# A selective scan's input products: the opening 128 tokens of a chunk by one full-array product

## The chip, the cores and the metric

The kernel runs on one core of one Trainium2 chip. The metric is the device time of one execution in microseconds (us), from three runs of the kernel before; the time of a changed kernel is compared with it. TensorE (PE) multiplies into PSUM, VectorE (DVE) runs the scans, ScalarE (ACT) the exponentials and copies, GpSimd (POOL) elementwise products and indirect transfers, SyncE (SP) issues the plain DMAs.

## What is computed

Input x is 2 x 2048 x 256, float32. Two layers, each with a layernorm ahead and a residual around it:

```
xn = layernorm(x)
B_t, C_t = xn W_B^T, xn W_C^T                 # 16 states n
dt  = softplus(xn W_dt1^T W_dt2^T + b)        # 256 channels d
A   = -exp(log_A);  A_bar = exp(dt * A)       # d x n
B_bar = (A_bar - 1) / (A + 1e-8) * xn * B_t
h_t = A_bar * h_(t-1) + B_bar                 # a scan over 2048 tokens for each d, n
y_t = sum_n h_t * C_t + D_skip * xn
x   = x + y
route = softmax(layernorm(x) Wr + br); e = argmax     # 8 experts
x   = x + gelu(layernorm(x) W1[e] + b1[e]) W2[e] + b2[e]
```

The kernel scans a shifted state, so that the input of its scan is w_t = u_t - u_(t+1), where u_t = xn_t * B_t[n]; a factor 1/(A + 1e-8) goes on C.

## The kernel before

The tokens are eight chunks (q = 0 to 7) of 512, four to a sequence; a chunk is four tiles (k = 0 to 3) of 128 tokens. Work in a chunk goes by sixteen units (n = 0 to 15); a unit m = 16q + n is two states of one half (128) of the channels, and thus two items g = 2m and 2m + 1, each 128 channels x 512 tokens. A unit passes these stages:

- `make_band` (POOL, L648): for each pair of units it multiplies a constant band (1 on the diagonal, -1 beside it, 65 wide, one for each 64 tokens) by the rows of B, for two states: 128 x 520, one operation. There are three such buffers.
- `make_w` (PE, L1055): w of the unit, 128 channels x (512 tokens x 2 states), in two PSUM banks. The stationary operand is xn of the tokens, the moving one the band. Each product covers 64 tokens, `product(r, k)`, where r is the upper or lower half of the array's rows, and writes 130 columns: two of them belong to the 64 tokens that follow, so they are added into PSUM on top of another product. Those with r = 0 use rows 0 to 63, those with r = 1 rows 64 to 127. `make_w(m, 0)` has five products (one of two columns alone), `make_w(m, 1)`, which waits for the end of the first part, has four: nine for a unit, each a float32 product of two instructions.
- `exp_a` (ACT, L835), A_bar of an item; `scan` (DVE, L1336), the recurrence, item by item, which reads w.
- multiplication with C (`make_hc`), on one of two engines: for a pooled item ACT copies C with its scale (`copy_C`, L825) and POOL multiplies (L667); for the others DVE does both in one operation from PSUM (L1355), a *VectorE pair*. `VECTOR_UNITS` lists which n of each chunk are VectorE pairs; sixteen of 128 units before.
- `add_y` (PE, L1093): four transposing products for each item, added up in PSUM (`YY`) over all items.

The four PSUM banks of `WW` hold two units, so PE's order in a chunk is, for each n: what `hops(q)` lists for n (small products for the next chunk, the router, or the skip term), then `make_w(m + 2)`, then `add_y` of the unit before the last. `make_w(m + 2)` waits until unit m's scans (or its VectorE pair) have freed the banks. All engines work through their queues in order.

`hops(q)` is a table: `xn0`, `xn1`, `bcd`, `brow`, `dt2_0`, `dt2_1` prepare chunk q + 1; `cbt`, `u_a`, `u01`, `u23` make the skip term; `xnr0`, `xnr1`, `routeT`, `route` the router of the chunk before; `early0`, `early1` (L1020) the token lists of the first four chunks, from which the first expert tiles are gathered while the last chunk still runs. `ODD`, `BANK` and `BEFORE` give each its shared PSUM bank and whose reader it has to wait for.

On SP, `chunk(q)` spreads a row of C over 128 partitions for every unit (`spread_C`, L497), six buffers ahead; in the last chunk at n = 9 it waits for `early1` and then issues three loads of W2 (L535), 512 KB each.

After the scan stage come 36 expert tiles (`hidden` L1172, `outputs` L1209), which are bound by PE alone.

Of the kernel before, what the change touches and what calls it, by code (L numbers as in the profile page):

```python
# [29 lines left out]
VECTOR_UNITS = [(4, 8, 12)] + [(5, 12)] * 4 + [(8,)] * 2 + [(4, 10, 15)]  # L30
# [9 lines left out]
BAND = 2 * (HALF + 1)  # L40
NR, NA, NH, NHC, NCS, NW, NB = 3, 4, 8, 8, 3, 4, 6
# [17 lines left out]
SMALL = dict(ident=P, logA=KD * N, wr=KD * CS, umask=1, wcd=KD * CBD, wdt2=D, skip=D, band=HALF + 1, last=1,  # L59
# [13 lines left out]
ODD = ("u01", "xn0", "bcd", "dt2_0", "dt2_1", "rank", "spread", "early0", "early1")  # L73
# [6 lines left out]
def hops(q):  # L80
# [121 lines left out]
def build(nc, x, small, w1, w2, b2, out):  # L202
    with ExitStack() as ctx:
# [38 lines left out]
        band_at = NR * TI * BAND  # L242
# [25 lines left out]
        bands = [b2_sb[:, i * TI * BAND:(i + 1) * TI * BAND].rearrange("p (i t) -> p i t", t=BAND) for i in range(NR)]  # L268
# [79 lines left out]
        most = max(b - a for a, b in BATCHES) * TI  # L348
# [3 lines left out]
        where = sb("where", [P, 3, most])  # L352
        lane = sb("lane", [P, 1])
# [117 lines left out]
        def _(eng):  # L471
# [28 lines left out]
            def chunk(q):  # L500
                for n in range(N):
# [75 lines left out]
        def _(eng):  # L577
# [184 lines left out]
        def _(eng):  # L762
# [75 lines left out]
            def emit(q):  # L838
                first, last, at = q == 0, q == NQ - 1, hops(q)
                for n in range(N):  # L840
# [23 lines left out]
                    if not first and n == (13 if last else 14):  # L864
                        softmax_exp(q - 1)
# [66 lines left out]
        def _(eng):  # L932
# [111 lines left out]
            def make_w(m, part):  # L1044
# [7 lines left out]
                def product(r, k, at=0, width=BAND, start=False):  # L1052
# [3 lines left out]
                                      band[rows, k, at:at + width], start=start, stop=not start, skip_group_check=True)  # L1056

                if part == 0:
# [7 lines left out]
                    product(0, 0, start=True)  # L1066
# [184 lines left out]
        def _(eng):  # L1251
# [178 lines left out]
            def place_tokens(batch, parts=(0, 1)):  # L1430
# [8 lines left out]
                if 0 in parts:  # L1439
# [418 lines left out]
```

## Time and profile before

| what | value |
|---|---|
| median of three runs | 726.18 us (724.6 to 726.65) |
| the profiled execution's own time | 726.01 us |
| its span, first to last instruction | 724.3 us |
| PE busy | 682.5 us, 94% |
| DVE, ACT, POOL busy | 538.0, 482.6, 485.6 us |
| mean granted clock of TensorE | 0.98 of full speed |

The span is one execution; busy time is what an engine's instructions took together, and a busy PE includes the latency of its pipeline. The scan stage takes the first 445 us or so, the experts the other 279 us. Granted clock 1.00 is TensorE at 2.4 GHz, 0.50 is 1.2 GHz. A view of the trace by windows has, in each row, the window (us from the span's start), its length, the busy us of the engines with the number of their instructions in brackets (in the order PE, PE's weight loads, DVE, ACT, POOL, or PE alone where a row is of one line's matmuls), the granted clock, the DMA engines' busy share and GB/s. The chunks are cut at the start of the w of a chunk's third unit, which is the first that PE makes within that chunk. In a group by line stand the busy us, the mean ns of one, and the idle time before them with what ended it.

### The profile page before, as it was taken

To read this page: it belongs to the slowest core of one execution; us is meant where nothing else is said; L and a number is where in the kernel's file an instruction comes from. 1 tells how busy PE (TensorE), PEld (TensorE's weight loads), DVE (VectorE), ACT (ScalarE), POOL (GpSimd) and SP (SyncE) were. 2 spreads that over 40 slices of the span, in tenths; PEclk is the share of its full clock that TensorE was granted. 3 is DMA by queue.
4 is the path that set the end of the run, shared out by engine and by line. 5 is a ranking of instruction groups with operands and counts; after the bars stand their busy time and mean duration, and the time that the engine had idled before them with its cause. 6 is when DMAs were issued, how large, how long until landed. Compare 5 with 4: busy or idle time off the path is not lost.

```text
span 724.3 us, 17510 instructions
## 1 busy us (share of the span) xinstructions
PE 682.5 (94%) x5826; PEld 574.6 (79%) x5827; DVE 538.0 (74%) x950; ACT 482.6 (67%) x1005; POOL 485.6 (67%) x616
## 2 busy tenths in 40 slices
PE   8899799999999998899998989999999999999997
PEld 7777677777787776678776778898999999977776
DVE  7799889989989989999999878887343333344441
ACT  3887999998998997899998586433232323233451
POOL 3889998998998987989989587233343434343331
PEclk9699999999999999999999799999999999999999
DMA  6787542342343243143242077711111111111010
GB/s 235 269 258 254 204 145 78 104 148 93 108 152 117 82 137 107 60 148 117 83 125 88 30 256 240 277 41 49 58 52 59 48 58 45 58 38 33 25 45 16
DMA packets 42290, 82.21 MB, mean 114 GB/s; under 512 B 4824, under 2 KB 12637, under 8 KB 42208
## 3 DMA queue, kind: packets, MB, share of 16 engines
q1 hardware_dynamic: 37600, 68.58, 28.7%
q0 software_dynamic: 4608, 12.59, 5.4%
q8 instruction: 45, 0.74, 0.4%
q14 instruction: 37, 0.30, 0.1%
HBM read 69.35 MB, written 13.37 MB: 114 GB/s over the span
## 4 chain that ended last, share of the span: by engine, by line
PE 58%; ACT 12%; POOL 9%; issue 7%; DVE 2%; DMA 1%; SPq 0%; POOLq 0%; ACTq 0%; DVEq 0%
PE WW L1172 16%; PE misc L1209 15%; PE WW L1055 10%; POOL w_sb L667 7%; PE YY L1093 7%; ACT w_sb L835 5%; ACT Csb L825 5%; PE misc L1204 2%; PE WW L1166 2%; DMA w_sb<-c_rows 1%; PE YY L1141 1%; PE misc L969 1%; ACT xin L805 1%; PE misc L981 1%; DVE w_sb L1336 1%
## 5 line engine op out<-in xcount | busy, mean ns | idle before, releaser
L667 POOL TENSOR_TENSOR w_sb<-w_sb,Csb 128x512 f32<-128x512 f32 x224 | 282.7, 1275 | 41.9 <-DVE w_sb L1336 37.7
L1055 PE MATMUL WW<-b_sb,xin 64*128 64x130 f32 (+2 forms) x2304 | 203.3, 293 | 23.4 <-DVE w_sb L1336 12.5
L1055 PEld LDWEIGHTS WW<-b_sb,xin 64*128 64x128 f32 x2304 | 168.4, 192 | 70.3 <-issue 30.6
L1336 DVE TENSOR_TENSOR_SCAN w_sb<-WW,hlast,w_sb 128x512 f32<-128x512 f32 x170 | 210.1, 1269 | 13.5 <-issue 6.5
L835 ACT ACTIVATE w_sb<-dt,negA 128x512 f32<-128x512 f32 x256 | 169.5, 709 | 4.0 <-DVE w_sb L1336 2.0
L916 ACT ACTIVATE dt<-WW,b1c 128x128 f32<-128x128 f32 x256 | 72.8, 387 | 129.2 <-PE WW L1172 129.0
L1093 PE MATMUL YY<-sm,w_sb 128*128 128x128 f32 x1024 | 142.4, 284 | 6.2 <-DVE row L1384 4.3
L729 POOL DMA_INDIRECT y_out<-CbX,ocol x36 | 42.6, 1184 | 142.0 <-DVE CbX L1758 137.3
L1093 PEld LDWEIGHTS YY<-sm,w_sb 128*128 128x128 f32 x1024 | 113.4, 143 | 21.2 <-issue 4.3
L825 ACT ACTIVATE Csb<-w_sb,invA 128x512 f32<-128x512 f32 x150 | 102.5, 713 | 23.2 <-POOL w_sb L667 21.5
L1209 PE MATMUL misc<-w_sb,dt 128*128 x512 | 115.7, 379 | 0.5 <-issue 0.5
L1209 PEld LDWEIGHTS misc<-w_sb,dt 128*128 128x128 f32 x512 | 94.9, 190 | 12.4 <-issue 0.7
L1172 PE MATMUL WW<-z,xin 128*128 128x128 f32 x512 | 99.2, 275 | 0.2
L1172 PEld LDWEIGHTS WW<-z,xin 128*128 128x128 f32 x512 | 78.4, 192 | 1.6 <-issue 0.7
L648 POOL TENSOR_TENSOR b_sb<-sm,brow 128x520 f32<-128x520 f32 x64 | 67.9, 1061 | 6.6 <-ACT brow L777 6.6
L1336 DVE TENSOR_TENSOR_SCAN w_sb<-WW,w_sb 128x512 f32<-128x512 f32 x54 | 63.8, 1208 | 7.2 <-ACT w_sb L835 3.5
L1758 DVE TENSOR_TENSOR CbX<-CbX,misc 128x256 f32<-128x256 f32 x36 | 15.1, 420 | 70.5 <-PE misc L1209 63.5
L825 ACT ACTIVATE Csb<-CbX,invA 128x512 f32<-128x512 f32 x74 | 50.8, 714 | 15.6 <-POOL w_sb L667 15.6
L1172 PE MATMUL WW<-z,xnT 128*128 128x128 f32 x288 | 55.9, 276 | 0.9 <-issue 0.9
L1172 PEld LDWEIGHTS WW<-z,xnT 128*128 128x128 f32 x288 | 44.5, 192 | 2.0 <-issue 1.5
L1172 PE MATMUL WW<-z,Csb 128*128 128x128 f32 x224 | 43.3, 275 | 0.0
L1638 DVE COPY z<-YY 128x256 f32<-128x256 f32 x34 | 14.3, 422 | 32.1 <-PE YY L1141 31.8
(304 smaller groups left out, 817.7 us busy)
## 6 DMA issues: line engine op xcount, KB each, us to landing
w_sb<-c_rows SPq DMA_DIRECT2D x86, 256.0 KB, 3.3
CbX<-c_rows SPq DMA_DIRECT2D x42, 256.0 KB, 3.3
w_sb<-w_in SPq DMA_DIRECT2D x20, 512.0 KB, 5.7
token_rows<-row SPq DMA_DIRECT2D x8, 1024.0 KB, 4.6
w_sb<-w_in SPq DMA_DIRECT2D x24, 256.0 KB
xin<-x_in SPq DMA_DIRECT2D x8, 512.0 KB, 3.8
w_sb<-x_in SPq DMA_DIRECT2D x7, 512.0 KB, 7.9
b_sb<-b_in SPq DMA_DIRECT2D x1, 780.0 KB, 8.3
```

What stands on the lines that cost most here:

```text
L648: eng.tensor_tensor(bands[pair % NR].rearrange("p i (t s) -> p i t s", s=2), col("band").unsqueeze(1).unsqueeze(3).to_broadcast([P, TI, HA ...
L667: eng.tensor_tensor(hc[g % NHC], hb_of(g), Csb[i % NCS][:, :], ALU.mult).then_inc(s_hcp, 1)
L729: eng.indirect_dma_start(out=outrows, out_offset=bass.IndirectOffsetOnAxis(ap=ocol[u][:, :], axis=0), in_=yo[u], in_offset=None, bounds_ch ...
L825: eng.activation(Csb[i % NCS][:, :], Cb[m % NB], ACT.Copy, scale=invA[:, h * N + n:h * N + n + 1])\
L835: eng.activation(A[g % NA], dts[q % B][:, h * TC:(h + 1) * TC], ACT.Exp, scale=negA[:, h * N + n:h * N + n + 1]).then_inc(s_a, 1)
L916: g = eng.activation(hT[u % 2][:, j * P:(j + 1) * P], hps[u % 2][:, j * P:(j + 1) * P], ACT.Gelu, bias=b1c[u][:, j:j + 1])
L1055: return eng.matmul(to[:, a:a + width], x_rows[rows, k, h * P:(h + 1) * P], band[rows, k, at:at + width], start=start, stop=not start, ski ...
L1093: mm = eng.matmul(YY[:, at:at + P], hc[g % NHC][:, i * P:(i + 1) * P], ident, is_transpose=True, start=(j == 0 and i % 2 == 0), stop=(j == ...
L1172: mm = eng.matmul(hps[u % 2][:, j * P:(j + 1) * P], w1c[u % 2][h][:, j * P:(j + 1) * P], xT[u % 2][:, h * P:(h + 1) * P], start=(h == 0), ...
L1209: mm = eng.matmul(yps[u % 2][:, 0:D], hT[u % 2][:, j * P:(j + 1) * P], w2_sb[:, bass.ds(e * KH * D + j * D, D)], start=(j == 0), stop=(j = ...
L1336: eng.tensor_tensor_scan(hb_of(g) if pooled(g) else w_of(g), w_of(g), A[g % NA], hlast[(q - 1) % 2][:, h * N + n:h * N + n + 1] if q % NC ...
L1758: eng.tensor_tensor(yo[u], yo[u], yps[u % 2][:, 0:D], ALU.add).then_inc(s_yo, 1)
```

## The change

1. **w.** The first tile (k = 0) of each unit is made by one product over all 128 rows, with a band 129 wide for two states, so 258 columns, in place of `product(0, 0)` and `product(1, 0)`. A unit has eight products now. Tiles 1 to 3 are as before.
2. **Bands.** `make_band` is two operations: 128 x 258 and, for the three other tiles, 128 x 390. The constants grow by 129 columns; `where` and `lane` move into columns that are no longer used.
3. **VectorE pairs.** 21 of 128 units in place of 16: chunks 1 to 3 have a third, chunks 5 and 6 a second; some of the numbers differ.
4. **Last chunk.** `early1` is ahead of the skip term (n = 3 and 4, before 6 and 7), `u` and the router come later; `keep_ids` on DVE is after item 11, before 17; the gathers go out at n = 8, 10, 12; SP's three loads stand at n = 11, 12, 13, one each. First `u_a` now waits for `keep_ids` too, as its bank is that of `early1`.
5. `place_tokens` and `first_table` are cut into other pieces, with the same operations but for one tensor less.

```diff
-VECTOR_UNITS = [(4, 8, 12)] + [(5, 12)] * 4 + [(8,)] * 2 + [(4, 10, 15)]
+VECTOR_UNITS = [(4, 8, 12)] + [(4, 8, 12)] * 3 + [(5, 12)] + [(4, 12)] * 2 + [(6, 11, 15)]
...
+WIDE = 2 * (P + 1)
+BANDS = WIDE + (TI - 1) * BAND
...
-ODD = ("u01", "xn0", "bcd", "dt2_0", "dt2_1", "rank", "spread", "early0", "early1")
+ODD = ("u01", "xn0", "bcd", "dt2_0", "dt2_1", "rank", "spread", "early0")
...
-        at = {1: [("cbt", q)], 3: [("u_a", q)], 4: [("u01", q), ("u23", q)], 6: [("early1_a", q)], 7: [("early1", q)],
-              8: [("xnr0", q - 1)], 9: [("xnr1", q - 1)], 10: [("routeT", q - 1)], 11: [("route", q - 1)],
-              13: [("turn", 0)]}
+        at = {1: [("cbt", q)], 3: [("early1_a", q)], 4: [("early1", q)], 6: [("u_a", q)], 7: [("u01", q), ("u23", q)],
+              9: [("xnr0", q - 1)], 10: [("xnr1", q - 1)], 11: [("routeT", q - 1)], 12: [("route", q - 1)],
+              14: [("turn", 0)]}
...
-                    if q == NQ - 1 and n == 9:
+                    if q == NQ - 1 and n in (11, 12, 13):
                         eng.wait_ge(s_full, HOP["early1", q] + 1)
-                        for i in range(17, 20):
-                            load_weights(i)
+                        load_weights(n + 6)
...
+                eng.tensor_tensor(wide_bands[pair % NR].rearrange("p (t s) -> p t s", s=2),
+                                  col("wide_band").unsqueeze(2).to_broadcast([P, P + 1, 2]),
+                                  brow[q % B][:, 0, N + 2 * p:N + 2 * p + 2].unsqueeze(1).to_broadcast([P, P + 1, 2]), ALU.mult)
                 eng.tensor_tensor(bands[pair % NR].rearrange("p i (t s) -> p i t s", s=2),
-                                  col("band").unsqueeze(1).unsqueeze(3).to_broadcast([P, TI, HALF + 1, 2]),
-                                  brow[q % B][:, :, N + 2 * p:N + 2 * p + 2].unsqueeze(2)
-                                  .to_broadcast([P, TI, HALF + 1, 2]), ALU.mult).then_inc(s_R, 1)
+                                  col("band").unsqueeze(1).unsqueeze(3).to_broadcast([P, TI - 1, HALF + 1, 2]),
+                                  brow[q % B][:, 1:, N + 2 * p:N + 2 * p + 2].unsqueeze(2)
+                                  .to_broadcast([P, TI - 1, HALF + 1, 2]), ALU.mult).then_inc(s_R, 1)
...
-                    if last and n in (9, 11, 13):
-                        t = (9, 11, 13).index(n)
+                    if last and n in (8, 10, 12):
+                        t = (8, 10, 12).index(n)
                         gather(t, t, 0)
...
-                    product(0, 0, start=True)
+                    eng.matmul(to[:, 0:WIDE], x_rows[:, 0, h * P:(h + 1) * P], wide_bands[pair % NR], start=True, stop=False,
+                               skip_group_check=True)
                     product(1, 2, start=True)
                     product(0, 1)
                     product(1, 3, width=2 * HALF)
...
                     eng.wait_ge(s_wf, m + 1)
                     product(0, 2)
-                    product(1, 0)
-                    product(0, 3)
-                    product(1, 1, width=2 * HALF).then_inc(s_wv, 2)
+                    product(1, 1, width=2 * HALF)
+                    product(0, 3).then_inc(s_wv, 2)
...
-                    if (j, gap) in (((9, 1), (11, 1)) if last else ((30, 0), (31, 0))):
-                        u_times_x(q, int(j in (11, 31)))
+                    if (j, gap) in (((15, 1), (16, 1)) if last else ((30, 0), (31, 0))):
+                        u_times_x(q, int(j in (16, 31)))
...
-                    if last and (j, gap) == (17, 0):
+                    if last and (j, gap) == (11, 0):
                         keep_ids()
```

How PE's order changes is shown at one unit in the middle of a chunk. `h_ready` is the wait for the scans that free the banks, `w_of_first_halves` the wait of the second part for the first. Before:

```order
L1006 MATMUL misc<-xnrT,sm 32x128 x7
L1055 MATMUL WW<-b_sb,xin 128x130 [waits h_ready]
L1055 MATMUL WW<-b_sb,xin 128x130 x2
L1055 MATMUL WW<-b_sb,xin 128x128
L1055 MATMUL WW<-b_sb,xin 128x2
L1055 MATMUL WW<-b_sb,xin 128x130 [waits w_of_first_halves]
L1055 MATMUL WW<-b_sb,xin 128x130 x2
L1055 MATMUL WW<-b_sb,xin 128x128
L1093 MATMUL YY<-sm,w_sb 128x128 [waits hC_ready_gpsimd]
```

and of the change:

```order
L1010 MATMUL misc<-xnrT,sm 32x128 x7
L1070 MATMUL WW<-b_sb,xin 128x258 [waits h_ready]
L1059 MATMUL WW<-b_sb,xin 128x130 x2
L1059 MATMUL WW<-b_sb,xin 128x128
L1059 MATMUL WW<-b_sb,xin 128x2
L1059 MATMUL WW<-b_sb,xin 128x130 [waits w_of_first_halves]
L1059 MATMUL WW<-b_sb,xin 128x128
L1059 MATMUL WW<-b_sb,xin 128x130
L1097 MATMUL YY<-sm,w_sb 128x128 [waits hC_ready_gpsimd]
```

The product of 258 columns stands ahead of the first part, in the place of one product of 130; the second part has lost one of 130.

On SP, the end of the last chunk's spreads of C (`c_rows`) and the three loads of W2 (`w_in`, 128x1024), before:

```order
L497 DMA w_sb<-c_rows 128x512 [waits C_copied,hC_ready] x2
L535 DMA w_sb<-w_in 128x1024 [waits shared_bank_filled]
L535 DMA w_sb<-w_in 128x1024 x2
L497 DMA w_sb<-c_rows 128x512 [waits C_copied,hC_ready] x2
L497 DMA CbX<-c_rows 128x512 [waits C_copied,hC_ready] x2
```

and of the change:

```order
L499 DMA w_sb<-c_rows 128x512 [waits C_copied,hC_ready] x4
L536 DMA w_sb<-w_in 128x1024 [waits shared_bank_filled]
L499 DMA CbX<-c_rows 128x512 [waits C_copied,hC_ready]
L536 DMA w_sb<-w_in 128x1024 [waits shared_bank_filled]
L499 DMA CbX<-c_rows 128x512 [waits C_copied,hC_ready]
L480 DMA token_rows<-row 128x4x512 [waits layernorm2_done]
L536 DMA w_sb<-w_in 128x1024 [waits shared_bank_filled]
```

Two more spreads go ahead of the first load, and the loads no longer stand in a row.

## Rows read from the trace of the kernel before

**Rows 1.** The page: busy times, and PE in 40 slices (tenths)

```profile
PE 682.5 (94%) x5826; PEld 574.6 (79%) x5827; DVE 538.0 (74%) x950; ACT 482.6 (67%) x1005; POOL 485.6 (67%) x616
...
PE   8899799999999998899998989999999999999997
```

**Rows 2.** Busy time of the engines in each chunk, q = 0 to 7

```profile
26.57:81.03 54.46, 50.89 (x449) 41.59 (x449) 47.97 (x69) 43.97 (x75) 51.27 (x74) 0.91 0.78 254
81.03:133.68 52.65, 48.36 (x475) 39.00 (x475) 48.69 (x58) 49.85 (x88) 48.91 (x59) 1.00 0.40 130
133.68:184.35 50.67, 48.10 (x475) 38.88 (x474) 47.03 (x57) 47.85 (x85) 46.91 (x57) 1.00 0.35 116
184.35:234.97 50.62, 48.09 (x475) 38.89 (x474) 46.97 (x55) 47.94 (x86) 45.14 (x45) 1.00 0.36 117
234.97:289.72 54.75, 50.09 (x477) 40.59 (x477) 49.15 (x75) 49.30 (x88) 47.05 (x58) 0.97 0.33 108
289.72:342.74 53.02, 49.24 (x483) 39.95 (x483) 51.98 (x71) 48.38 (x85) 49.67 (x61) 1.00 0.35 111
342.74:395.47 52.73, 49.42 (x483) 39.99 (x482) 50.73 (x82) 49.20 (x87) 49.45 (x59) 1.00 0.31 102
395.47:445.00 49.53, 43.66 (x403) 36.98 (x404) 41.85 (x52) 35.72 (x58) 36.94 (x39) 0.90 0.46 150
```

**Rows 3.** Chain of waits in q = 3: start us, us, what

```profile
194.16 0.78 PE WW L1055 x10
...
194.98 0.72 PE WW L1055 x8
195.69 1.02 PE YY L1093 x8
196.72 0.86 PE misc L969 x2
```

**Rows 4.** Windows of 0.11 us, matmuls alone: L1055 (w), L1093 (`add_y`)

```profile
231.42:231.53 0.11, 0.10 (x2) 1.00 1.18 419
...
232.96:233.07 0.11, 0.10 (x1) 1.00 0.74 279
```

**Rows 5.** Timeline of PE's weight loads, end of `add_y`, start of w

```profile
233.90 0.91 PEld L1093 LDWEIGHTS YY<-sm,w_sb 128*128 128x128 f32 x8
234.97 0.30 PEld L1055 LDWEIGHTS WW<-b_sb,xin 64*128 64x128 f32 x4 [0.17 <-issue]
```

**Rows 6.** Windows around the stretches at a low clock

```profile
22.00:37.00 15.00, 13.21 (x83) 11.56 (x85) 11.73 (x15) 13.38 (x24) 13.93 (x20) 0.54 0.77 261
281.00:291.00 10.00, 8.19 (x69) 7.23 (x71) 9.51 (x20) 6.80 (x13) 6.59 (x9) 0.83 0.39 131
397.00:409.00 12.00, 10.64 (x62) 8.57 (x60) 10.34 (x20) 7.04 (x11) 6.01 (x5) 0.57 0.15 45
```

**Rows 7.** Groups by line, and who waited for L648

```profile
L667 POOL TENSOR_TENSOR w_sb<-w_sb,Csb 128x512 f32<-128x512 f32 x224 | 282.7, 1275 | 41.9 <-DVE w_sb L1336 37.7 <-ACT Csb L825 3.3 <-PE misc L998 0.5
L1336 DVE TENSOR_TENSOR_SCAN w_sb<-WW,hlast,w_sb 128x512 f32<-128x512 f32 x170 | 210.1, 1269 | 13.5 <-issue 6.5 <-PE WW L1055 6.5
L648 POOL TENSOR_TENSOR b_sb<-sm,brow 128x520 f32<-128x520 f32 x64 | 67.9, 1061 | 6.6 <-ACT brow L777 6.6
L1355 DVE SCALAR_TENSOR_TENSOR w_sb<-WW,invA,w_sb 128x512 f32<-128x512 f32 x22 | 15.8, 734 | 1.8 <-issue 1.3 <-DMA w_sb<-c_rows 0.5
L640 POOL TENSOR_TENSOR blast<-brow,sm 128x16 f32<-128x16 f32 x8 | 1.7, 216 | 0.0
...
  PEld WW L1055: 6.2, 7
```

**Rows 8.** Chain of waits in q = 7, and the page's DMA issues

```profile
420.80 0.38 SPq L497
421.28 8.79 DMA w_sb<-c_rows
...
w_sb<-c_rows SPq DMA_DIRECT2D x86, 256.0 KB, 3.3
```

More of the change, by code:

```diff
@@ L56 @@
 EPS = 1e-5
-SMALL = dict(ident=P, logA=KD * N, wr=KD * CS, umask=1, wcd=KD * CBD, wdt2=D, skip=D, band=HALF + 1, last=1,
+SMALL = dict(ident=P, logA=KD * N, wr=KD * CS, umask=1, wcd=KD * CBD, wdt2=D, skip=D, band=HALF + 1, wide_band=P + 1, last=1,
              b1=E * KH, tri=P, br_row=1, e_less8=E, e_base=E, tok0=NT, j128=32, tile_no=ENTRIES - SURE, turned=2 * len(SPLIT))
@@ L266, in build @@
         Csb = [Csbs[:, i * TC:(i + 1) * TC] for i in range(NCS)]
-        bands = [b2_sb[:, i * TI * BAND:(i + 1) * TI * BAND].rearrange("p (i t) -> p i t", t=BAND) for i in range(NR)]
+        wide_bands = [b2_sb[:, i * BANDS:i * BANDS + WIDE] for i in range(NR)]
+        bands = [b2_sb[:, i * BANDS + WIDE:(i + 1) * BANDS].rearrange("p (i t) -> p i t", t=BAND) for i in range(NR)]
         brow = [sb(f"brow{b}", [P, TI, 2 * N])[:, :, :] for b in range(B)]
@@ L351, in build @@
         counted = sb("counted", [P, (E + 1) * CAP], BF16)
-        where = sb("where", [P, 3, most])
-        lane = sb("lane", [P, 1])
+        where = col("logA").rearrange("p (a k) -> p a k", a=2)
+        lane = col("tri", 33, 34)
         spare = sm[:, OFF["wcd"][0]:OFF["skip"][1]]
@@ L863, in emit @@
                         copy_first_W1()
-                    if not first and n == (13 if last else 14):
+                    if not first and n == 14:
                         softmax_exp(q - 1)
@@ L1055, in product @@
                     return eng.matmul(to[:, a:a + width], x_rows[rows, k, h * P:(h + 1) * P],
-                                      band[rows, k, at:at + width], start=start, stop=not start, skip_group_check=True)
+                                      band[rows, k - 1, at:at + width], start=start, stop=not start, skip_group_check=True)
                 if part == 0:
@@ L1428, in choose, with place_tokens @@
                     eng.tensor_tensor(onehot[:, 0:tiles, :], over_e(top), less8, ALU.is_equal).then_inc(s_oh, 1)
-            def place_tokens(batch, parts=(0, 1)):
+            def place_tokens(batch, parts=(0, 1, 2)):
                 q0, q1 = BATCHES[batch]
@@ L1444, in place_tokens @@
                     done(eng.tensor_copy(totals[:, :, 0:1], before), "rt")
+                if 1 in parts:
+                    keep = z[1][:, 256:256 + E * (tiles + 1)]
                     done(eng.tensor_tensor_scan(runs[batch], keep,
                                                 ranks[:, 128:128 + (tiles + 1) * E], 0.0, ALU.mult, ALU.add), "rt")
-                if 1 not in parts:
+                    done(eng.tensor_tensor(slot, slot, run[batch][:, :, 0:tiles].rearrange("p e i -> p i e"), ALU.add), "rt")
+                if 2 not in parts:
                     return
-                done(eng.tensor_tensor(slot, slot, run[batch][:, :, 0:tiles].rearrange("p e i -> p i e"), ALU.add), "rt")
                 done(eng.tensor_tensor(slot, slot, onehot[:, 0:tiles, :], ALU.mult), "rt")
                 done(eng.tensor_reduce(slotf, slot, AX.X, ALU.add), "rt")
-                row_at, column, sum_at = (where[:, i, 0:tiles] for i in range(3))
-                done(eng.tensor_scalar(sum_at, slotf, 1.0 / P, -(P - 1) / (2.0 * P), ALU.mult, ALU.add), "rt")
-                done(eng.tensor_scalar(column, sum_at, ROUND, None, ALU.add), "rt")
+                row_at, column = (where[:, i, 0:tiles] for i in range(2))
+                done(eng.tensor_scalar(column, slotf, 1.0 / P, -(P - 1) / (2.0 * P), ALU.mult, ALU.add), "rt")
+                done(eng.tensor_scalar(column, column, ROUND, None, ALU.add), "rt")
                 done(eng.tensor_scalar(column, column, ROUND, None, ALU.subtract), "rt")
@@ L1557, in between @@
                             aggregate(1, q - 1)
-                        if (j, gap) == ((24, 0) if last else (26, 0)):
+                        if (j, gap) == (26, 0):
                             logits(q - 1)
@@ L1566, in between @@
                     if q == BATCHES[0][1] + 1 and j == 2:
-                        place_tokens(0, (gap,))
+                        place_tokens(0, (1, 2) if gap else (0,))
                     if q in (NQ - 3, NQ - 2) and gap and j in range(10, 26, 2):
@@ L1571, in between @@
                         keep_half()
-                    if last and 0 <= 2 * j + gap - 2 <= 4:
-                        first_table(2 * j + gap - 2)
-                    if last and (j, gap) == (17, 0):
+                    if last and gap and j <= 4:
+                        first_table(j)
+                    if last and (j, gap) == (11, 0):
                         keep_ids()
-                    if last and (j, gap) == (28, 1):
+                    if last and (j, gap) == (30, 0):
                         eng.wait_ge(s_full, HOP["turn", 0] + 1)
@@ L1824 @@
     band[one, one % HALF + 1] = -1.0
+    wide_band = np.zeros((P, P + 1), f)
+    wide_band[one, one] = 1.0
+    wide_band[one, one + 1] = -1.0
     parts = dict(
```

5 lines of the change are left out of this document (2 added, 3 removed).

## The prediction, as it was put on record

> **What bounds the kernel now.** I read the page's head first [rows 1]: PE is busy in 94% of the span, and its line of tenths stands at 8 or 9 through nearly all of the scan stage; the others have a quarter to a third of the span free, which could lie anywhere. So I cut the scan stage into its chunks, each from the start of the w of a chunk's third unit to the next one's [rows 2]. In the two calmest, q = 2 and 3, PE is busy 48.1 of 50.6 us, while DVE has 47.0, ACT 47.9 and POOL 46.9 or less. All four are nearly full, PE most. What span less PE's busy time leaves is 3.6, 4.3, 2.6, 2.5, 4.7, 3.8, 3.3 and 5.9 us for the eight rows: 30.6 us in all. The chain of waits [rows 3] says the same: from 194 us on, for half a chunk, it stays on PE without a step to another engine: a unit of L1055 (0.78 and 0.72 us, 1.54 with the step between them), the `add_y` of two items (1.02 us), a product for the next chunk (L969), and again. Only the other half of a chunk leads over POOL and ACT. In such a stage, each us put on PE beyond its idle 30.6 us is a us of the time.
>
> **The wide product.** Today the nine products of a unit run two at a time. The slots of 0.11 us show it [rows 4]: in the first one of a unit two half-array instructions have begun, where one full-array instruction of `add_y` fills the same slot. Eight of the nine products, two instructions each, thus take eight slots, and that is the 1.54 us with a weight load and the wait between the parts. The rows 0 to 63 have four products, the rows 64 to 127 four and the one of two columns.
>
> After the change the full product has no partner. What it costs can be read off a full-array float32 product, L969 [rows 3]: its two instructions of 512 columns take 0.86 us, 0.84 ns for each column and instruction. For two instructions of 258 columns: 2 x 258 x 0.84 = 0.434 us. What does it save? Nothing of length. In part one `product(0, 0)` goes, but its partner (1, 2) stays, then (1, 3) and the two columns, all three on the upper rows, so part one is as long as before. In part two (1, 0) goes, but (0, 2) and (0, 3) must follow each other on the lower rows: two products long, as before. A unit is thus 0.434 us longer, and it is 18 instructions less 2.
>
> Around a run of half-array products there is a gap: PE's weight loads stop 0.17 us before it, while the eight full-array loads ahead go on without one [rows 5]. The change moves this gap from between `add_y` and w to between the wide and the first half product, and I cost the move at nothing. A page of the Trainium skill, "TensorE: Matmul & The Clock Gate", section The mechanism, has PE pull a weight load ahead of running products when it goes to other rows of the array or to the background buffer. The trace shows this among full-array loads, and has the 0.17 us in its place before half-array ones; by the rule the sum would be nearer to that of rival B, 731 us, which stands below with its own rows.
>
> Sum for 128 units: 128 x 0.434 = **+55.5 us** of PE time. Some units at the start run at half clock (0.54 over 22 to 37 us [rows 6]), four of them, at twice the price: **+1.7**.
>
> **Bands.** POOL's operation of 128 x 520 takes 1061 ns, one of 128 x 16 takes 216 [rows 7]: 1.68 ns an element and 189 fixed. So 258 and 390 elements come to 622 + 843 = 1465 ns, +0.40 us for a pair, 64 x 0.40 = 25.9 us of POOL. Against it five units fewer on POOL, ten products of 1275 ns: -12.8. In chunks 1 to 3, +3.2 - 2.6 = +0.6 on 46 to 49 us; in chunk 0, which gets no VectorE pair, 51.3 + 3.2 = 54.5. Both hide under PE's chunk of 55 us and more; if PE were not longer, the cover would be gone at once. The first band lies ahead of the first w: **+0.4**.
>
> **VectorE pairs.** Five more: ten operations of 734 ns [rows 7], +7.3 us of DVE, and ACT has ten copies less. DVE's fullest chunk, q = 5, goes from 52.0 to 53.5 us, again under PE's. They hold the banks of their unit 1.5 us longer; `make_w` of the unit after the next waits for that. With a unit of PE time now 3.4 us (a chunk of 55 us over 16), the two scans and two products of DVE, 2 x 1.27 + 2 x 0.73 = 4.0 us, end before PE is back at those banks, which is two units later. Nothing.
>
> **What comes back.** PE's idle time is where others are late for it, and a slower PE finds them ready. Some stays: at the end of a chunk `YY` has to be emptied, and the small products wait for ACT's copies. Between all 30.6 us and nothing I keep 1.2 us a chunk, half of what the calmest has: 30.6 - 8 x 1.2 = **-21**. In it is the last chunk's stall: SP issues three loads of 512 KB in a row, and the C that it spreads behind them takes 8.8 us to land, where the page's median is 3.3 [rows 8]. The change puts them apart.
>
> The clock falls to half at three places [rows 6]. Over 397 to 409 us it is 0.57 on average: 10.3 us at half speed, less 1.4 idle, half of it lost: 4.5. Over 281 to 291 us it is 0.83: 3.4 us, half of it less the idle, 1.2. In both chunks PE waits most of all [rows 2], and I take it that a PE that waits less keeps its clock: **-5.7**. The one at 22 us, when PE waits for the first units, stays.
>
> **Last chunk.** `early1`, the gathers and `keep_ids` come earlier, the router's hops later; all are the same instructions. The new wait of `u_a` is for an operation that DVE does right after item 11, whose scan the `make_w` ahead of `u_a` waits for anyhow: nothing. The expert stage starts with what it started with: nothing.
>
> **Sum.** 55.5 + 1.7 + 0.4 - 21 - 5.7 = +30.9 on the profiled execution's 726.0 us: 756.9, say **757 us**. That execution is within 0.2 us of the median of 726.18, so the two need no correction.
>
> **The rivals.**
> A, the forecast: PE bound, 757 us, 745 to 766 by what comes back. For it: [rows 2 to 4]. Chance 0.66.
> B, the wide product costs half as much. The gap [rows 5] is worth 0.17 us, and about 0.2 with what the load behind it takes beyond a slot: the wide one's own load can run under `add_y`, and if the half-array loads run under the wide product too, the price is 0.434 - 0.2 = 0.23, 128 x 0.23 = 30, and the time 757 - 25.6 = 731. Against it: no weight load of a half-array product stands under a full one in the rows. Above it everything up to A is open. Chance 0.15.
> C, POOL's bands come late. PE already waits 6.2 us, seven times, for a band [rows 7]; the operation is 0.40 us longer 64 times. If half of these land on PE: 770; if all: 783. Against it: POOL gets 6 us a chunk of slack from PE. Chance 0.14.
> D, faster. PE isn't the bound but one of four in a ring, and its waits are set by the late POOL: then five units fewer on POOL, the clock that doesn't fall and the last chunk's loads count, and the wide product goes into idle time and into both its gaps (two of 0.17 us, [rows 5], so 0.1 us are left of the price, 128 x 0.1 = 13 us). 726 + 13 + 2 - 5.7 - 12 (of the idle time only what POOL set, its ten products) = 723 us. It decides if the price is under about 0.13 us a unit. Against it: the half chunk on PE alone [rows 3]. Chance 0.05.
> That the change doesn't do what it says is excluded for w: PE's order has the 258 columns in every unit.
>
> **The numbers.** The range leaves out D, half of C and the lowest of B: **732 to 772 us**. A measurement of this kernel tells 0.3% (about 2 us) from no change. Slower by more than that: A, B and C with hardly a remainder, 0.93; faster 0.05; the same 0.02.
>
> **What would show it.** The chunk rows: 55 to 57 us for q = 2 and 3, PE busy 54 or more of them, the other engines' busy times nearly as before. The w of a unit: 1.97 us from its first weight load to the next `add_y`; for B 1.75. POOL's two operations of some 0.62 and 0.84 us. Clock at 1.00 in q = 4 and at the start of q = 7. C shows as waits of PE for the band of over 10 us. The prediction is wrong if the chunk stays at 51 us: either the wide product is cheap (see its length), or PE had more time than its busy rows say.

## The result, and the profile after

The change takes **770.23 us** (median of 4 runs, 767.62 to 770.91) against 726.4 us of the kernel before (4 runs, 724.6 to 726.65): a ratio of **1.0586**, 95% interval 1.0547 to 1.0626. That is 44 us slower, where 31 were forecast. The profiled execution took 769.91 us, its span 768.1 us, 43.8 more than before.

The page of the change, to be set beside [rows 1]:

```profile
PE 743.5 (97%) x5570; PEld 608.1 (79%) x5571; DVE 548.2 (71%) x964; ACT 481.0 (63%) x995; POOL 496.8 (65%) x666
...
PE   8899999999999999899999999999999999999997
...
PEclk9599999999999999999999999999999999999999
```

PE is busy 61.0 us more with 256 instructions fewer; DVE has 10 us more, POOL 11, ACT 2 less. Where the time lies is seen by chunks. I cut both kernels once more at one and the same place, the start of w of the unit m = 16q + 2 ([rows 2] stand up to a unit later in some chunks). Before, q = 0, 4, 5, 6 and 7 (q = 2 and 3 are as in [rows 2]; q = 1 is 52.67 us, the experts 279.75):

```profile
22.86:77.46 54.60, 50.49 (x433) 40.97 (x434) 48.31 (x70) 44.57 (x77) 50.97 (x72) 0.88 0.78 252
...
231.43:284.22 52.79, 48.40 (x477) 39.05 (x476) 47.61 (x65) 47.99 (x84) 46.91 (x57) 1.00 0.37 120
284.22:338.30 54.08, 50.02 (x475) 40.59 (x475) 52.74 (x81) 49.39 (x86) 48.91 (x61) 0.97 0.31 100
338.30:390.22 51.92, 50.25 (x492) 40.88 (x491) 50.28 (x72) 49.09 (x87) 49.56 (x61) 1.00 0.35 114
390.22:444.55 54.33, 46.77 (x435) 39.65 (x434) 46.17 (x65) 39.62 (x64) 40.82 (x43) 0.91 0.44 146
```

The change, q = 0, q = 2 to 7, and the expert stage (q = 1 is 57.81 us):

```profile
23.26:83.98 60.72, 59.77 (x400) 46.20 (x401) 49.67 (x71) 45.56 (x76) 54.11 (x80) 0.86 0.69 224
...
141.79:199.23 57.44, 56.01 (x444) 43.41 (x443) 48.66 (x60) 47.32 (x83) 47.37 (x63) 1.00 0.33 102
199.23:256.61 57.38, 56.02 (x445) 43.42 (x444) 48.52 (x57) 47.26 (x83) 45.50 (x50) 1.00 0.32 103
256.61:314.99 58.38, 56.48 (x447) 43.71 (x446) 47.41 (x65) 47.77 (x83) 49.14 (x65) 1.00 0.33 103
314.99:376.83 61.84, 59.07 (x441) 46.13 (x442) 55.71 (x84) 49.35 (x85) 50.54 (x67) 0.94 0.27 92
376.83:435.79 58.96, 57.83 (x461) 45.17 (x459) 52.61 (x77) 48.62 (x85) 49.29 (x66) 1.00 0.30 96
435.79:488.31 52.52, 49.08 (x409) 39.57 (x408) 45.62 (x62) 39.10 (x63) 43.97 (x49) 1.00 0.52 162
488.31:768.10 279.79, 273.96 (x1910) 241.79 (x1908) 134.80 (x375) 96.94 (x338) 98.08 (x138) 1.00 0.20 64
```

The change is longer by 0.4 us ahead of q = 0 (23.26 and 22.86), by 6.1, 5.1, 6.8, 6.8, 5.6, 7.8, 7.0 and -1.8 in q = 0 to 7, and by 0.04 in the expert stage: together 43.8. In q = 2 PE is busy 56.01 us where it was 48.11, +7.90, and idle 1.43 where it was 2.57: +6.76 in all. Over the whole scan stage PE's busy time grew by 61.0 us and its idle time fell from 36.0 to 18.8 (over q = 0 to 7 alone, from 31.2 to 14.8).

The chain of waits of the change in q = 5, which answers to [rows 3]:

```profile
338.13 0.43 PE WW L1070 x2
338.56 0.77 PE WW L1059 x8
339.33 0.04 issue
339.38 0.71 PE WW L1059 x6
340.09 1.02 PE YY L1097 x8
341.11 0.36 PE misc L980 x4
341.47 0.63 PE WW L1070 x2
```

A unit was 0.78 + 0.04 + 0.72 and 1.02 of `add_y`; it is now 0.43 + 0.77 + 0.04 + 0.71 and 1.02. Two half-array products fewer made neither part shorter by more than 0.01 us. So the unit is 0.43 us longer, as the forecast's 0.434. The last line is what the forecast didn't have: after a small product of its own tiling (L980, `brow`) the wide product shows 0.63 us.

The groups of POOL's two band operations, of the change:

```profile
L649 POOL TENSOR_TENSOR b_sb<-sm,brow 128x258 f32<-128x258 f32 x64 | 39.5, 617 | 6.6 <-ACT brow L781 6.6
L652 POOL TENSOR_TENSOR b_sb<-sm,brow 128x390 f32<-128x390 f32 x64 | 53.9, 843 | 0.0
```

617 and 843 ns were forecast as 622 and 843.

### The profile page after: what moved, and what is told of

It reads as the page before. It is cut to its first block, busy times and chain, and to the rows that moved or that the text cites. A ratio compares the mean times of both kernels' runs of the same rounds, so it can differ in the third digit from the quotient of the medians.

```text
span 768.1 us, 17039 instructions
## 1 busy us (share of the span) xinstructions
PE 743.5 (97%) x5570; PEld 608.1 (79%) x5571; DVE 548.2 (71%) x964; ACT 481.0 (63%) x995; POOL 496.8 (65%) x666
## 4 chain that ended last, share of the span: by engine, by line
PE 81%; POOL 6%; issue 5%; DVE 5%; ACT 2%; POOLq 0%; DVEq 0%; ACTq 0%
PE WW L1059 19%; PE WW L1176 15%; PE misc L1213 14%; PE YY L1097 12%; PE WW L1070 7%; POOL w_sb L671 4%; PE misc L1208 2%; PE WW L1170 2%; DVE w_sb L1340 2%; PE misc L985 2%; PE misc L973 1%; PE YY L1145 1%; PE misc L941 1%; ACT Csb L829 1%; ACT w_sb L839 1%
## 5 line engine op out<-in xcount | busy, mean ns | idle before, releaser
L671 POOL TENSOR_TENSOR w_sb<-w_sb,Csb 128x512 f32<-128x512 f32 x214 | 270.5, 1274 | 71.9 <-DVE w_sb L1340 67.3
L1340 DVE TENSOR_TENSOR_SCAN w_sb<-WW,hlast,w_sb 128x512 f32<-128x512 f32 x160 | 199.3, 1271 | 26.1 <-PE WW L1059 25.5
L1059 PEld LDWEIGHTS WW<-b_sb,xin 64*128 64x128 f32 x1792 | 165.2, 190 | 62.6 <-issue 44.5
L1059 PE MATMUL WW<-b_sb,xin 64*128 64x130 f32 (+2 forms) x1792 | 201.1, 297 | 7.2
L829 ACT ACTIVATE Csb<-w_sb,invA 128x512 f32<-128x512 f32 x144 | 99.7, 715 | 48.8 <-POOL w_sb L671 48.5
L1070 PE MATMUL WW<-b_sb,xin 128*128 128x258 f32 x256 | 84.7, 413 | 7.7 <-DVE w_sb L1340 6.4
L1070 PEld LDWEIGHTS WW<-b_sb,xin 128*128 128x128 f32 x256 | 40.9, 195 | 29.1 <-issue 21.9
L829 ACT ACTIVATE Csb<-CbX,invA 128x512 f32<-128x512 f32 x70 | 48.2, 714 | 15.3 <-POOL w_sb L671 15.1
L652 POOL TENSOR_TENSOR b_sb<-sm,brow 128x390 f32<-128x390 f32 x64 | 53.9, 843 | 0.0
L1340 DVE TENSOR_TENSOR_SCAN WW<-WW,hlast,w_sb 128x512 f32<-128x512 f32 x32 | 40.2, 1279 | 13.6 <-PE WW L1059 13.6
```

What stands on the lines that cost most here:

```text
L671: eng.tensor_tensor(hc[g % NHC], hb_of(g), Csb[i % NCS][:, :], ALU.mult).then_inc(s_hcp, 1)
L829: eng.activation(Csb[i % NCS][:, :], Cb[m % NB], ACT.Copy, scale=invA[:, h * N + n:h * N + n + 1])\
L1059: return eng.matmul(to[:, a:a + width], x_rows[rows, k, h * P:(h + 1) * P], band[rows, k - 1, at:at + width], start=start, stop=not start, ...
L1070: eng.matmul(to[:, 0:WIDE], x_rows[:, 0, h * P:(h + 1) * P], wide_bands[pair % NR], start=True, stop=False, skip_group_check=True)
L1340: eng.tensor_tensor_scan(hb_of(g) if pooled(g) else w_of(g), w_of(g), A[g % NA], hlast[(q - 1) % 2][:, h * N + n:h * N + n + 1] if q % NC ...
```

## The experiments

Each kernel is compared with the kernel before, run on the same chip beside it. "As before" in an edit means the text of the kernel before.

**e1, the wide product and the two band operations alone.** The change with the pairs and the last chunk as before:

```diff
-VECTOR_UNITS = [(4, 8, 12)] + [(4, 8, 12)] * 3 + [(5, 12)] + [(4, 12)] * 2 + [(6, 11, 15)]
+VECTOR_UNITS = [(4, 8, 12)] + [(5, 12)] * 4 + [(8,)] * 2 + [(4, 10, 15)]
...
-        at = {1: [("cbt", q)], 3: [("early1_a", q)], 4: [("early1", q)], 6: [("u_a", q)], 7: [("u01", q), ("u23", q)],
+        at = {1: [("cbt", q)], 3: [("u_a", q)], 4: [("u01", q), ("u23", q)], 6: [("early1_a", q)], 7: [("early1", q)],
```

> The change's wide product and its bands in two operations, with the VectorE pairs and the last chunk's order of the kernel before. Theory P (PE sets the pace, each unit is 0.434 us longer, and PE's spare time is all that gives): the pairs are worth little under a longer PE, so about the changed kernel's 770 us, 768 to 778 with the last chunk's stall back. Theory Q (the four engines form a ring in which POOL counts as much): POOL has 26 us more in bands and no relief, so 785 us or more.

Measured: 767.28 us, ratio 1.0582 (1.0490 to 1.0675), 40 us over before's 726.99 there. Its chunks q = 2 and 5:

```profile
141.89:198.67 56.78, 55.78 (x445) 43.50 (x444) 47.39 (x57) 48.54 (x86) 50.12 (x66) 1.00 0.32 103
...
313.83:373.19 59.36, 56.05 (x442) 43.51 (x443) 54.00 (x81) 50.82 (x88) 53.53 (x70) 1.00 0.30 98
```

This lies just under the 768 to 778 us of theory P and far from Q's 785. Parts 1 and 2 of the change are nearly all of its 44 us. q = 2 is 0.66 us shorter than in the change, though POOL has more to do: the third pair costs something there.

**e2, the rest alone.** The change with nine half-array products and one band operation, pairs and order kept:

```diff
-                    eng.matmul(to[:, 0:WIDE], x_rows[:, 0, h * P:(h + 1) * P], wide_bands[pair % NR], start=True, stop=False,
-                               skip_group_check=True)
+                    product(0, 0, start=True)
...
-                    product(0, 3).then_inc(s_wv, 2)
+                    product(1, 0)
+                    product(0, 3)
```

> The changed kernel without the wide product: nine half products and one band operation as before, but its VectorE pairs, order and last chunk. P: the 770 us lose 55.5 us of products and some 8 us of gaps around small products, and the idle time of PE comes back: 718 to 726 us. Q: with POOL relieved of 13 us and no longer bands, clearly below the kernel before, 715 us or less.

Measured: 740.04 us, ratio 1.0171 (1.0110 to 1.0232). Slower by 1.1 to 2.3%, where either theory had it no slower than before: both missed. That called for the two halves of the rest by themselves.

**e3, the last chunk's order alone**, put into the kernel before:

```diff
-                    if q == NQ - 1 and n == 9:
+                    if q == NQ - 1 and n in (11, 12, 13):
                         eng.wait_ge(s_full, HOP["early1", q] + 1)
-                        for i in range(17, 20):
-                            load_weights(i)
+                        load_weights(n + 6)
```

> The kernel before with the last chunk's new order alone (early lists ahead of u, loads of W2 apart, gathers earlier, pieces of place_tokens as before). P and Q: the stall behind the three loads, 2.6 us of PE waits, goes: 722 to 725 us. A rival: the first u products now wait for the lists on DVE, and nothing is gained, 726 to 728 us.

Measured: 726.01 us, ratio 0.9977 (0.9949 to 1.0006). The gain of 2 to 4 us that both theories had did not come; the rival, that nothing is gained, fits. In its profile q = 7 is 52.30 us instead of 54.33 and q = 6 52.64 instead of 51.92, and no engine waits for a spread of C any more, where ACT waited 1.5 us before. What the stall of [rows 8] was worth is at the edge of what these runs tell, 1 us or so.

**e7, the pairs alone**, put into the kernel before:

```diff
-VECTOR_UNITS = [(4, 8, 12)] + [(5, 12)] * 4 + [(8,)] * 2 + [(4, 10, 15)]
+VECTOR_UNITS = [(4, 8, 12)] + [(4, 8, 12)] * 3 + [(5, 12)] + [(4, 12)] * 2 + [(6, 11, 15)]
```

> The kernel before with the changed list of VectorE pairs alone. In the run with half products, the pairs and the new order it took 740 us, with the new order alone 726. Theory V (each further pair keeps its PSUM banks and VectorE 1.5 us longer, and PE waits for most of it): the pairs are the whole of that, 735 to 741 us. Rival: the pairs only cost together with the new order's pieces: 728 to 731 us.

Measured: 741.97 us, ratio 1.0216 (1.0188 to 1.0244). PE's waits for DVE's pairs, before and then here:

```profile
PE WW L1055 <- DVE w_sb L1355: 3.0, 4, 1.1
```

```profile
PE WW L1055 <- DVE w_sb L1355: 8.1, 12, 1.0
```

and its chunks q = 2, 6 and 7:

```profile
132.02:184.27 52.25, 48.14 (x475) 38.94 (x474) 48.29 (x60) 46.86 (x82) 44.37 (x55) 1.00 0.34 112
...
346.40:404.50 58.10, 53.22 (x491) 43.28 (x490) 52.19 (x75) 48.42 (x84) 46.95 (x58) 0.94 0.32 101
404.50:463.26 58.76, 49.24 (x434) 41.95 (x434) 46.84 (x65) 39.80 (x63) 42.05 (x44) 0.85 0.43 139
```

With half-array products the new list costs 16 us: in q = 2 1.5 us of PE's idle time, though POOL is 2.5 us less busy, and in q = 5 to 7 a granted clock of 0.94, 0.94 and 0.85 where it was 0.97, 1.00 and 0.91. The list has five pairs more, and some of the old ones stand at other places. In q = 7, which has three as before and is 4.4 us longer, only the places differ. No run separates number and place. This profiled execution took 744.86 us, the longest of the four, so its dips are at the upper end.

**e8, fewer pairs**, in the kernel before, one in q = 1 to 4 instead of two:

```diff
-VECTOR_UNITS = [(4, 8, 12)] + [(5, 12)] * 4 + [(8,)] * 2 + [(4, 10, 15)]
+VECTOR_UNITS = [(4, 8, 12)] + [(8,)] * 6 + [(4, 10, 15)]
```

> The kernel before with one VectorE pair in chunks 1 to 4 in place of two. V: if a pair costs PE what the third one cost (1.4 us in each of chunks 2 and 3), four fewer give 720 to 724 us. Rival: GpSimd, with 2.6 us more in chunks where it has 45 to 49 of 51 to 53, becomes the bound: 728 to 735 us.

Measured: 726.4 us, ratio 1.0028 (0.9989 to 1.0068): neither theory holds. POOL goes to 49.5 us in q = 2, and that chunk is 51.26 us, 0.6 longer. In its profile q = 1 to 5 are 1.6 us longer in all, and q = 7, whose pairs are as before, is 2.4 us shorter at a clock of 0.93 where it was 0.91. So fewer pairs gained nothing in the chunks that lost them, and the total says less than these rows.

**e4, the wide product issued twice**, the same into the same place (`start=True` both times, so the result is that of one):

```diff
-                    eng.matmul(to[:, 0:WIDE], x_rows[:, 0, h * P:(h + 1) * P], wide_bands[pair % NR], start=True, stop=False,
-                               skip_group_check=True)
+                    for _ in range(2):
+                        eng.matmul(to[:, 0:WIDE], x_rows[:, 0, h * P:(h + 1) * P], wide_bands[pair % NR], start=True,
+                                   stop=False, skip_group_check=True)
```

> The changed kernel with each unit's wide product issued twice (the second overwrites the first, so nothing else changes). P: each unit is 2 x 258 columns longer, 128 x 0.434 = 55.5 us: 822 to 828 us. Q: PE's addition is partly taken up by waits that PE has now (14.8 us), and by POOL's idle time: 800 to 812 us.

Measured: 815.12 us, ratio 1.1188 (1.1105 to 1.1271), 45 us over the change and between the ranges of the two theories: P had 55 us more. In the profiles PE's busy time grew by 51.4 us (794.86 and 743.50), and PE's idle time fell by 5.8, as a longer PE finds more of the others ready. Its q = 2:

```profile
155.75:219.37 63.62, 62.70 (x476) 49.58 (x475) 49.12 (x60) 48.21 (x83) 47.24 (x61) 1.00 0.29 93
```

PE is busy 6.69 us more in a chunk, 0.418 us a unit, and idle 0.92 us. Chunk and PE's work now differ by 1.5%: nothing else bounds a middle chunk. A wide product beside its like shows no gap.

**e5, the wide band made twice**, with a semaphore between, so that POOL has 64 operations of 0.62 us more:

```diff
+                own["n"] += 1
+                eng.wait_ge(s_eps, own["n"])
+                eng.tensor_tensor(wide_bands[pair % NR].rearrange("p (t s) -> p t s", s=2),
```

> The changed kernel with the 128x258 band operation done twice for each pair, so 64 x 0.62 = 40 us more on GpSimd. Theory P (TensorE sets the pace): GpSimd's chunks of 45 to 50 us grow by 5 us and stay under the 57.4 us of a chunk; only chunk 0, where GpSimd has 54.1 us already, can grow: 769 to 774 us. Theory C (late bands hold PE): 785 us or more.

Measured: 776.58 us, ratio 1.0712 (1.0679 to 1.0744), 6 us over the change for 37 us more on POOL. That is 2.6 us above the range of P and 8 below what C had at least.

```profile
24.41:86.27 61.86, 59.96 (x401) 46.15 (x402) 48.94 (x70) 45.23 (x76) 57.19 (x87) 0.87 0.67 214
86.27:145.67 59.40, 57.65 (x442) 45.07 (x442) 49.42 (x60) 48.37 (x84) 55.05 (x74) 0.97 0.36 127
145.67:203.12 57.45, 56.02 (x445) 43.40 (x443) 48.65 (x60) 47.10 (x82) 52.07 (x71) 1.00 0.31 101
```

q = 2 is 57.45 us as it was 57.44, with POOL at 52.07, and q = 3 and 4 grew by 0.01 us each. What is paid is paid elsewhere: 1.15 us ahead of q = 0, where the weight load of the first w waits 1.5 us for its band instead of 0.8, 1.1 and 1.6 us in q = 0 and 1, where POOL comes to 57 and 55 us, 0.5 and 0.8 in q = 5 and 6, and 1.4 in q = 7 at a clock of 0.97 instead of 1.00. Bands once, at 47 us of POOL, cost nothing in the middle chunks.

**e6, the small products behind w.** In the change the hops in part of the array (`u_a`, `u01`, `u23`, `brow`, `routeT`) are issued after `make_w`, so that they stand beside half-array products, as the wide one no longer follows them:

```diff
+                    tiled = ("u_a", "u01", "u23", "brow", "routeT")
...
-                        fill(*hop)
+                        if hop[0] not in tiled:
+                            fill(*hop)
...
+                    for hop in at.get(n, ()):
+                        if hop[0] in tiled:
+                            fill(*hop)
```

> The changed kernel with the small products that use a part of the array's rows or columns (u_a, u01, u23, brow, routeT) behind the unit's w in place of ahead of it. Theory G (each change between full and part-array products costs PE 0.2 us, and the wide product made one more of them at these places): four a chunk fewer, 0.8 us a chunk, 6 us in all, 762 to 766 us. Rival: what waits for these products gets them 2.2 us later and the gain is lost, 769 us or more.

Measured: 780.27 us, ratio 1.0753 (1.0714 to 1.0791). PE is busy 0.49 us less in q = 2 (55.52), but the chunk is 57.93 us long; the readers of the small products wait (`ACT z` for L1010 18.0 us where it was 6.1, `DVE tail` for L941 25.1 where it was 5.3), DVE's scans come late behind them, and PE's waits for scans are

```profile
PE WW L1070 <- DVE w_sb L1345: 15.2, 13, 2.9
```

where the change has 6.4 us, 7 times. The rival was right, and theory G's 0.8 us a chunk came to 0.49: the place of these products is worth more than the gap.

**The change once more, and three neighbours on the same chip.** e12 is the change itself, with no edit:

> The changed kernel once more, on the chip of the three runs beside it, to compare them with: 768 to 772 us.

Measured: 769.62 us, ratio 1.0564 (1.0499 to 1.0629), with the same chunks (57.44 and 57.37 us for q = 2 and 3, clock 0.94 in q = 5).

e9 is the change with the pairs of before:

```diff
-VECTOR_UNITS = [(4, 8, 12)] + [(4, 8, 12)] * 3 + [(5, 12)] + [(4, 12)] * 2 + [(6, 11, 15)]
+VECTOR_UNITS = [(4, 8, 12)] + [(5, 12)] * 4 + [(8,)] * 2 + [(4, 10, 15)]
```

> The changed kernel with the VectorE pairs of before, so the wide product, the bands and the last chunk's order. The wide product alone took 767.3 us. Theory V (a further pair costs PE waits even in a chunk that PE bounds: 57.4 against 56.8 us in chunks 2 and 3): 763 to 767 us, and below the changed kernel. Rival: the pairs pay for themselves on GpSimd's side, 769 us or more.

Measured: 766.81 us, ratio 1.0535 (1.0472 to 1.0598), 2.8 us under the change beside it, as theory V had it. The chunks with added pairs (q = 1, 2, 3, 5 and 6) are 2.0 us of it in the profiles. Its q = 2 and 5:

```profile
140.70:197.48 56.78, 55.79 (x445) 43.49 (x444) 47.39 (x57) 48.54 (x85) 50.13 (x66) 1.00 0.32 103
...
312.63:374.54 61.91, 59.13 (x441) 46.21 (x442) 54.22 (x81) 50.92 (x88) 53.48 (x70) 0.94 0.29 93
```

Against e1 this is telling: up to the last chunk both have the same instructions in the same order, and q = 2 is the same to 0.01 us. But q = 5 took 61.91 us at a clock of 0.94 here and 59.36 at 1.00 there. So the dip in q = 5 isn't made by the added pairs, nor by anything else in which these two differ; an execution of one and the same work shows it or doesn't. (q = 0 tells the same: 59.34 us at 0.88 here, 60.88 at 0.86 there.)

e10 has the wide product behind the half-array ones, to give the unit one boundary with `add_y` as before:

```diff
-                    product(0, 1)
+                    product(0, 1, start=True)
...
-                    product(0, 3).then_inc(s_wv, 2)
+                    product(0, 3)
+                    eng.matmul(to[:, 0:WIDE], x_rows[:, 0, h * P:(h + 1) * P], wide_bands[pair % NR], start=False, stop=True,
+                               skip_group_check=True).then_inc(s_wv, 2)
```

> The changed kernel with the wide product behind the half products of its unit in place of ahead of them; the small products stay where they are. Theory G (a change between full and part of the array costs 0.2 us): two changes a unit as before, but at the four small part-array products of a chunk one fewer: PE busy 0.8 us less in a chunk, 763 to 767 us. Rival: the cost sits elsewhere (the wide product's own weights, the wait between the parts), and nothing changes, 769 to 772 us.

Measured: 767.45 us, ratio 1.0545 (1.0481 to 1.0609), 2.2 us under the change. Its chain in q = 3:

```profile
210.93 0.81 PE WW L1059 x8
211.78 0.71 PE WW L1059 x6
212.50 0.63 PE WW L1079 x2
213.13 0.87 PE YY L1097 x8
```

The wide product shows 0.63 us in every unit, `add_y` 0.87 instead of 1.02: the gap has moved with it. A unit is 0.77 + 0.04 + 0.71 + 0.63 + 0.87 = 3.02 us where the change has 2.98, and sixteen times this takes back 0.6 of theory G's 0.8 us; 0.23 us a chunk is all that PE is less busy. e11 has both, e10 with the pairs of before:

```diff
-VECTOR_UNITS = [(4, 8, 12)] + [(4, 8, 12)] * 3 + [(5, 12)] + [(4, 12)] * 2 + [(6, 11, 15)]
+VECTOR_UNITS = [(4, 8, 12)] + [(5, 12)] * 4 + [(8,)] * 2 + [(4, 10, 15)]
```

> Both of the last two: wide product last, VectorE pairs of before. V and G together: 757 to 762 us, which is what the forecast had for the change; if it is below 757, more than these two was missed.

Measured: 765.35 us, ratio 1.0514 (1.0451 to 1.0578), 3 us above the expected range. It is 4.3 us under the change, where e9 and e10 gained 2.8 and 2.2: the two parts nearly add up, but G's was forecast at twice what it gives. It is the quickest of those with a wide product, and none of them comes near the kernel before.

## Why the prediction was right, and where it fell short

The forecast named the result: slower, with PE as the bound, and the runs show that mechanism. That the number lies in the range of 732 to 772 us is in part luck. Rival A, the forecast's own account, had 757 us and at most 766; 770 is inside only because the range left room for half of C, whose late bands these runs do not show. The time was 13 us above 757, and the steps show where.

**What bounds the kernel: right.** 97.5% of a middle chunk is PE's after the change (56.01 of 57.44 us), 98.5% with the product doubled.

**The wide product: right in both halves.** Its price of 0.434 us (unit 0.43 longer; 0.418 by doubling), and that the two half-array products it replaces save nothing, since their partners stay. With the bands it makes 40 of the 44 us (e1).

**"I cost the move at nothing": wrong in part.** Between `add_y` and the unit it holds. But four small products in a chunk (L980, L1010, two of L941) are tiled themselves. Ahead of half-array products they ran into w without a loss; ahead of a full-array one they leave a gap, 0.63 us instead of 0.44, and L990 half of that: 4 x 0.19 + 0.09 = 0.85 us a chunk. 6.94 for the sixteen wide products and 0.85 make 7.79 of the 7.90 us by which PE's busy time grew; eight chunks, about 7 us. The chain has one more such place in each chunk: where one unit's w follows another's with no `add_y` between them, the wide product behind half-array ones shows 0.63 too (148.00 us), and with it the sum is 7.98, so it holds to 0.1 us only. That these are what the rows show is a reading of the chain; the two kernels that moved the small products or the wide one took 0.49 and 0.23 us of the 0.85 off PE's busy time, so the place of the gap was shown only in part.

The weight load: by the rule of the Trainium skill that is cited there, the time would have been nearer 731 us. The timeline of the change has no load of a half-array product under the wide one:

```profile
198.41 0.85 PEld L1097 LDWEIGHTS YY<-sm,w_sb 128*128 128x128 f32 x8
199.23 0.30 PEld L1070 LDWEIGHTS WW<-b_sb,xin 128*128 128x128 f32 x2
199.87 0.74 PEld L1059 LDWEIGHTS WW<-b_sb,xin 64*128 64x128 f32 x8 [0.33 <-issue]
```

The wide one's two loads follow those of `add_y` at once; the half-array ones stop for 0.33 us, nearly as long as the wide one's columns still run. The trace decided for the row, and against B.

**Bands: right.** The two operations to within 5 ns, and hidden where POOL has 47 us (e5). C was to show as waits of PE for the band of over 10 us; there is one, of 0.8 us, of the weight loads.

**"VectorE pairs ... Nothing": wrong.** e9 beside the change puts the new list at 2.8 us with the wide product, e7 at 16 us without. In the change's q = 2 the chain leaves PE at the pair that was added (n = 4):

```profile
151.19 0.73 DVE st L1266 x2
151.92 1.19 DVE WW L1340
...
153.34 0.41 DVE st L1266
153.75 1.19 DVE WW L1340
154.94 0.10 DVE w_sb L1359
...
155.64 0.67 DVE w_sb L1359
156.31 0.14 issue
156.44 0.67 PE WW L1070 x2
```

My 4.0 us for two scans and two pair operations left out what DVE does between them, here the statistics of the router's layernorm for the chunk before (L1266, 0.73 and 0.41), and its register work. From the first of these lines to the bank's release it is 5.1 us, and PE waits 0.4 us at it; the chunk is 0.66 us longer than in e9. The 3.4 us of a PE unit, twice, were no cover, as DVE doesn't start with the unit. DVE's busy time rose by 10.3 us where 7.3 were forecast; 3.3 of it are there without the added pairs (e1, 541.24 and 537.95).

**What comes back, -21: too much.** The idle time kept is 14.8 us, not 9.6. q = 0 to 4 and 6 keep 0.9 to 1.9 us (1.2 forecast), but q = 5 keeps 2.8 and q = 7 3.4.

**The clock, -5.7: half right.** Each dip has to be looked for at the same work, not at the same time. The one over 281 to 291 us in [rows 6] stands, before, where DVE makes the token lists at the turn from q = 4 to q = 5:

```profile
285.28 0.16 DVE z L1442
```

In the change these lists begin at 316.05 us, and the dip is there still, and longer: q = 5 has a clock of 0.94 where it had 0.97. So this dip did not go, but grew. The forecast's sign, 1.00 in q = 4, tells nothing in the rows above: they are cut earlier than [rows 2], and in them the kernel before has 1.00 in q = 4 too. 22 to 37 us stayed, as forecast (0.53). The windows around the lists in the change:

```profile
314.00:322.00 8.00, 5.50 (x44) 4.22 (x42) 7.58 (x16) 5.95 (x11) 6.16 (x7) 1.00 0.36 128
322.00:330.00 8.00, 7.67 (x40) 6.45 (x39) 8.00 (x13) 4.64 (x9) 6.91 (x10) 0.57 0.23 66
```

PE is idle 2.5 of 8 us there, 1.6 of them (319 to 321 us) for scans that stand behind 3.4 us of token lists on DVE (L1446 to L1462, in the chain from 316.05 to 319.48), and then runs at half. e1 has the same wait (idle 1.6 us from 318 to 320) and kept 1.00; PE is busy 3.0 us more in the change's q = 5 than there. So the dip was a term of 3 us that an execution can show or not. Of the twelve experiments e4 and e6 too stand at 1.00 in q = 5, the nine others at 0.94 to 0.97. I had taken it that a PE that waits less keeps its clock; in sum it waits less, but a single wait as long as this one stayed, as the token lists are DVE's own and not PE's pace.

The dip in q = 7 is gone in this execution (1.00 where it was 0.91). In e12, the same kernel, q = 7 has 0.97, with PE busy 1.65 us more, so of the 4.5 us forecast there an execution gives back all or a part.

**Last chunk.** q = 7 is 1.8 us shorter although its units are longer. The stall did go: ACT waits 2.0 us for spreads of C in e1, which has the order of before, and nothing waits for them in the change. But that is not what made the chunk shorter. e1's q = 7 and that of e12, the change once more:

```profile
431.63:485.76 54.13, 50.58 (x409) 40.88 (x407) 46.36 (x63) 38.80 (x62) 41.67 (x47) 0.97 0.44 145
```

```profile
435.10:489.27 54.17, 50.73 (x409) 41.17 (x408) 45.74 (x62) 39.31 (x63) 43.91 (x49) 0.97 0.48 157
```

At the same clock the old and the new order take the same time, and PE is idle 3.55 and 3.44 us. The 1.8 us come from the clock, 1.00 instead of 0.91, and from idle time that a longer PE takes up in either order. For the whole, e3 gives nothing that can be told, and e9 beside e1 (766.81 and 767.28) the same.

**The 12.9 us that the profiled execution was over the sum.** PE's busy time grew by 61.0 us, where 55.5 + 1.7 - 5.7 = 51.5 were forecast: 9.5 over, of which the gaps are about 7 and the dip in q = 5 3. Its idle time fell by 17.2, where 20.6 (21 less the 0.4 ahead of the first w) were forecast: 3.4 over. Of both the new list of pairs carries 2.8 us (e9).

**The rivals.** B is refuted by the 0.43 us, C by e5 in the middle chunks, D by e1 and by e4, where a second wide product adds its whole stream to a chunk's PE time. But D held something: without the wide product the engines are coupled closely, and it had the sign wrong. The list that takes work off POOL and gives it to DVE made that kernel 16 us slower (e7), and taking pairs from DVE made it no faster (e8).

## What to carry to other kernels

A half-array product that runs beside another cost nothing of its own here, so count what a change leaves in each half: taking one of each of two pairs away saved no time, and a full-array product in their place cost its whole stream. Where the full-array one touches products of another tiling, add the gap on that side too, for each neighbour it gets, small ones included. Before work moves to an engine with room in its sum, follow one buffer through that engine's queue in the trace, with all that stands between the two operations that free it; slack on average is no cover for one long wait, and the clock may fall behind it. And before a stretch of the trace is called gone, look for it at the same instructions: a window at the old time holds other work once the kernel has become longer.

## What was not expected of the hardware

A full-array float32 product of 258 columns (two instructions) behind products in a part of the array shows 0.63 us in the chain, and 0.44 behind a full-array one; with the wide product last in the unit (e10) every one shows 0.63. The other was that two kernels with the same instructions up to that point, e1 and e9, differ by 2.55 us in one chunk, at a granted clock of 1.00 and 0.94. In the change's dip, pieces of the chain take 1.20, 1.39 and 1.90 us (two instructions of L1070, eight of L1059, `add_y`) that take 0.44, 0.77 and 1.02 at 2.4 GHz.
